# Two heads per slot, q in two f16 parts, and fewer DMAs for the attention rows of a fused attention and FFN block

## What is computed

```python
x = L0_attn_x                                  # (16, 256, 128) f32
xn = _layernorm(x, axis=-1)
x = x + attn(xn, ...) + ffn(xn, ...)
# attn: 16 heads of 8 dims, for each of the 16 batches
q, k, v = (split_heads(einsum('bsh,oh->bso', xn, w) * s + b) for each of q, k, v)
attn = softmax(einsum('bhqd,bhkd->bhqk', q, k) / sqrt(8), axis=-1)
ctx = einsum('bhqk,bhkd->bhqd', attn, v)       # then merged and sent through w_o, s_o, b_o
# ffn: three dense layers with weights of +1 and -1, 256(x, -x) -> 512 -> 512 -> 128
h = relu(s0 * h @ W0) * 2; h = relu(s1 * h @ W1) * 2; h = s2 * h @ W2
```

## Time and profile before

| what | us |
|---|---|
| median of three runs | 345.76 (343.56 to 347.13) |
| the profiled execution | 348.12 |
| its span, first to last instruction | 346.3 |
| busy: PE, DVE, ACT, POOL | 310.8, 281.3, 237.1, 107.5 |

### The profile page before, as it was taken

The page is one execution under the profiler, slowest core; times in us unless marked ns, Lnnn a source line. Parts: engine busy times, 40 slices in busy tenths (PEclk is TensorE's granted clock), DMA queues, the critical chain, the costliest instruction groups (busy, mean ns, idle before and its releaser), DMA issues.

```text
span 346.3 us, 9162 instructions
## 1 busy us (share of the span) xinstructions
PE 310.8 (90%) x3248; PEld 174.2 (50%) x3248; DVE 281.3 (81%) x655; ACT 237.1 (68%) x515; POOL 107.5 (31%) x186
## 2 busy tenths in 40 slices
PE   5957789998999999999999998999989999997792
PEld 5734445454554555564555545455645555553331
DVE  4737778888988898888989888988889988988722
ACT  2314286877778696968677785968777786956771
POOL 2332323323242432433232424324222424300000
PEclk9978989999999999999999999999999999999987
DMA  4231314031322313141313223131413223130001
GB/s 122 59 96 40 91 39 112 22 108 38 89 76 64 103 48 102 48 116 35 99 49 85 82 61 103 43 109 42 114 27 100 66 77 88 42 107 4 19 3 31
DMA packets 28415, 23.88 MB, mean 69 GB/s; under 512 B 5698, under 2 KB 25170, under 8 KB 28370
## 3 DMA queue, kind: packets, MB, share of 16 engines
q1 hardware_dynamic: 28370, 23.29, 25.1%
HBM read 15.47 MB, written 7.34 MB: 66 GB/s over the span
## 4 chain that ended last, share of the span: by engine, by line
PE 41%; SPq 26%; DMA 13%; ACT 7%; issue 6%; POOL 3%; DVE 3%; POOLq 0%; ACTq 0%; DVEq 0%
SPq L360 12%; PE st_bank L846 12%; PE ctx_bank L880 10%; DMA q_rows<-max_rows 10%; SPq L365 7%; PE work L938 5%; PE work L908 5%; PE work L894 4%; SPq L352 3%; DMA q_rows<-q_scratch 3%; SPq L392 3%; POOL q_part L325 3%; ACT probs L502 2%; PE work L928 2%; ACT q_part L556 2%
## 5 line engine op out<-in xcount | busy, mean ns | idle before, releaser
L502 ACT ACTIVATE probs<-st_bank 128x512 f32<-128x512 f32 x248 | 148.7, 603 | 67.8 <-PE st_bank L846 64.7
L647 DVE TENSOR_REDUCE neg_max<-s_bank 128x2 f32<-128x512 f32 x248 | 168.5, 683 | 25.3 <-PE s_bank L853 23.0
L846 PE MATMUL st_bank<-q_rows,k_rows 51*128 51x256 bf16 x496 | 94.3, 274 | 15.5 <-DMA q_rows<-max_rows 9.9
L853 PE MATMUL s_bank<-k_rows,q_rows 48*128 48x256 f16 x496 | 95.8, 276 | 3.9 <-DMA q_rows<-q_scratch 3.9
L880 PE MATMUL ctx_bank<-probs,v_ext 128*32 128x256 f32 x1024 | 69.8, 391 | 1.2 <-ACT probs L502 1.2
L846 PEld LDWEIGHTS st_bank<-q_rows,k_rows 51*128 51x128 f16 x496 | 28.9, 94 | 70.7 <-issue 34.3
L901 PE MATMUL work<-r_hi,w 128*128 128x256 f16 x256 | 59.6, 274 | 3.8 <-DVE r_lo L618 2.2
L901 PE MATMUL work<-r_lo,w 128*128 128x256 f16 x256 | 59.2, 272 | 0.0
L722 DVE STREAM_TRANSPOSE turned<-ctx_bank 128x256 f32<-128x256 f32 x64 | 28.6, 446 | 22.3 <-PE ctx_bank L880 21.1
L618 DVE SCALAR_TENSOR_TENSOR r_lo<-work,r_hi 128x512 f16<-128x512 f32 x64 | 43.5, 681 | 3.9 <-ACT r_hi L491 3.8
L491 ACT ACTIVATE r_hi<-work 128x512 f16<-128x512 f32 x64 | 38.3, 602 | 11.4 <-PE work L901 9.8
(11 more groups left out here) (97 smaller groups left out, 393.1 us busy)
## 6 DMA issues: line engine op xcount, KB each, us to landing
k_rows<-k_scratch SPq DMA_DIRECT2D x64, 96.0 KB
q_rows<-q_scratch SPq DMA_DIRECT2D x64, 96.0 KB
q_scratch<-q_part SPq DMA_DIRECT2D x48, 64.0 KB, 2.0
xin<-x SPq DMA_DIRECT2D x16, 128.0 KB, 2.1
k_scratch<-k_part SPq DMA_DIRECT2D x32, 64.0 KB, 2.0
out<-outs SPq DMA_DIRECT2D x16, 128.0 KB, 1.8
q_rows<-max_rows SPq DMA_DIRECT2D x64, 6.0 KB
w_sb<-w SPq DMA_DIRECT2D x1, 256.0 KB, 2.6
```

Of the source, the lines that this page charges most:

```text
L502: nc.scalar.activation(probs[head // GROUP % 2][:, head % GROUP, :, :].rearrange("p k q -> p (k q)"), exp_banks(s)[t % len(exp_banks(s))][ ...
L647: nc.vector.tensor_reduce(out=neg_max[:, t // HALF, t % 2, t % HALF // 2, :], in_=max_banks(s)[t % len(max_banks(s))][:, :].rearrange("p ( ...
L846: return mm(banks[t % len(banks)][:, kt * SEQ:(kt + 1) * SEQ], k[:, kt * P:(kt + 1) * P], q, start=True, stop=True)
L853: return mm(banks[t % len(banks)][:, qt * SEQ:(qt + 1) * SEQ], q[:, qt * P:(qt + 1) * P], k, start=True, stop=True)
```

## The change

- **Two heads a slot.** A step has 8 slots `j`. PE writes the scores of heads 2j and 2j+1 of lag 2 into one pair of banks `st_pair`, then those of lag 1 into one pair `s_pair`. ACT and DVE read 1024 elements at once. While both lags exist there is one pair for each, written again in the next slot once its reader is done; in steps with one lag only, two pairs alternate. The slot tables are gone, the work is written out by slot.
- **q in two f16 parts**, scaled by powers of two that are worked out from the weights at the start (`row_scales`, now some 17 small DVE operations and one more matmul of PE between them). Rows are 8 x 2 x 2 = 32, with maxima 34. Exp takes its scale from a tile.
- **Splits.** DVE casts q and k hi in one operation of 128 x 512, POOL subtracts both lo in one. ACT makes no parts.
- **DMAs.** Four stores (k and q of hi, then of lo) and four loads of 32 rows, all loads behind all stores. The x load stands ahead of `store_max` of half 1.
- **Maxima.** Three small operations on POOL, two f16 parts, 16 maxima rows for 2 row DMAs' sources.
- **Contexts.** Groups 0 and 1 lie side by side in the bank and are transposed at once (128 x 512), and so 2 and 3.

```diff
-QPARTS, KPARTS = 3, 2
-ROWS = DH * QPARTS * KPARTS
-MROWS = ROWS + QPARTS
+PARTS = 2
+ROWS = DH * PARTS * PARTS
+MROWS = ROWS + PARTS
...
+QUARTER = HALF // 2
+HROWS = PARTS * QUARTER * TT
...
-    q_scratch = nc.dram_tensor("q_scratch", (2 * DH, QPARTS, HALF, SEQ), bf16, kind="Internal").ap()
-    k_scratch = nc.dram_tensor("k_scratch", (2 * DH, KPARTS, HALF, SEQ), f16, kind="Internal").ap()
+    q_scratch = nc.dram_tensor("q_scratch", (2 * DH, PARTS, HALF, SEQ), f16, kind="Internal").ap()
+    k_scratch = nc.dram_tensor("k_scratch", (2, PARTS, DH, HALF, SEQ), f16, kind="Internal").ap()
...
+        def split_qk(s, engine, eng):
+
+            s.wait(eng, hi_ready, 1, 0, 1)
+            s.wait(eng, lo_stored, 16 * 2, 1, 16 * 2)
+            engine.tensor_tensor(qk_part[:, 1, :, :], qk[:, :, :], qk_part[:, 0, :, :], ALU.subtract
+                                 ).then_inc(lo_ready, 1)
...
                     s.wait(sp, rows_loaded, LOADS, 1, LOADS)
-                    for part, ready in ((0, k_hi_ready), (1, k_lo_ready)):
+                    for part, ready, stored in ((0, hi_ready, hi_stored), (1, lo_ready, lo_stored)):
                         s.wait(sp, ready, 1, 0, 1)
...
+                        sp.dma_start(k_scratch[:, part].rearrange("x d e t -> x (d e) t"), qk_part[:, part, 1, :]
+                                     ).then_inc(stored, 16)
+                        sp.dma_start(q_scratch[:, part], qk_part[:, part, 0, :]).then_inc(stored, 16)
+
+                    s.wait(sp, hi_stored, 32, 0, 32)
+                    s.wait(sp, lo_stored, 32, 0, 32)
+                    s.wait(sp, st_psum, HALF, 3, HALF)
+                    for par in range(2):
+                        k_src = k_scratch[par:par + 1].rearrange("x b d e t -> (b d) x (e t)")
+                        sp.dma_start(k_rows[s.third(0)][par * TILE:par * TILE + ROWS, :],
+                                     k_src.to_broadcast([PARTS * DH, PARTS, COLS])).then_inc(rows_loaded, 16)
+                    for par in range(2):
+                        q_src = q_scratch[par * DH:(par + 1) * DH].rearrange("d (x a) e t -> x (d a) (e t)", x=1)
+                        sp.dma_start(q_rows[s.third(0)][par * TILE:par * TILE + ROWS, :],
+                                     q_src.to_broadcast([PARTS, PARTS * DH, COLS])).then_inc(rows_loaded, 16)
...
+            def scores_for_exp(s, j):
+
+                if j % QUARTER == 0:
+                    s.wait(pe, max_rows_loaded[j // QUARTER], MAX_LOADS, 2, MAX_LOADS)
+                pairs = exp_pairs(s)
+                s.wait(pe, probs_ready, HALF, 2, j if j == 0 else j + 1 - len(pairs))
...
+                dst = pairs[j % len(pairs)]
+                for kt in range(TT):
+                    for par in range(2):
+                        q, k = (rows_of(rows, s.third(2), 2 * j + par, MROWS) for rows in (q_rows, k_rows))
+                        c = (TT * par + kt) * SEQ
+                        last = mm(dst[:, c:c + SEQ], k[:, kt * P:(kt + 1) * P], q, start=True, stop=True)
+                last.then_inc(st_psum, 1)
+
+            def scores_for_max(s, j):
+
+                if j == 0:
+                    s.wait(pe, rows_loaded, LOADS, 1, LOADS)
+                pairs = max_pairs(s)
+                s.wait(pe, max_ready, HALF, 1, j + 1 - len(pairs))
...
+            def split_max(s, lag, half):
+
+                full, part = neg_max[:, half], max_part[:, half]
+                s.wait(pool, max_ready, HALF, lag, QUARTER * (half + 1))
+                s.wait(pool, maxT_psum, 2, lag + 1, half + 1)
...
+                    if j == 1 and s.has(3):
+                        turn_context(s, 3, 1)
...
                         nc.vector.reciprocal(rden[:, :, :], turned[:, :, :, DH]).then_inc(rden_ready, 1)
...
+                    if j == 1 and s.has(0):
+                        s.wait(dve, qk_scaled, 2, 0, 2)
+                        s.wait(dve, hi_stored, 32, 1, 32)
+                        s.wait(dve, lo_ready, 1, 1, 1)
+                        nc.vector.tensor_copy(qk_part[:, 0, :, :], qk[:, :, :]).then_inc(hi_ready, 1)
...
+                    if j == 2 and s.has(0):
+                        s.wait(dve, l1_psum, 2, 1, 2)
+                        for k, name in enumerate(("l0a", "l0b")):
+                            s.wait(dve, r0_hi_ready, 2, 0, k + 1)
+                            relu_lo(k, psum(name), r0_hi, r0_lo, r0_ready)
```

More of the change, by code:

```diff
@@ L61 @@
 TURN = 32
[L68 to L82, removed]
+BANK = {"xT": 0, "qk": 0, "l0b": 0, "l1a": 0, "v": 0, "max1": 1, "l0a": 1, "l1b": 1, "l2": 2, "max0": 2, "o": 2}
 class Step:
@@ L502, in step @@
                         nc.scalar.activation(
-                            probs[head // GROUP % 2][:, head % GROUP, :, :].rearrange("p k q -> p (k q)"),
-                            exp_banks(s)[t % len(exp_banks(s))][:, :], ACT.Exp, scale=EXP_SCALE).then_inc(probs_ready, 1)
-                    if t == ACT_SLOT["ffn"] and s.has(1):
+                            probs[j // 2 % 2][:, j % 2 * 2:j % 2 * 2 + 2, :, :].rearrange("p h k q -> p (h k q)"),
+                            pairs[j % len(pairs)][:, :], ACT.Exp, scale=exp_scale[:, :]).then_inc(probs_ready, 1)
@@ new lines, in step @@
+                    if j == 0 and s.has(0):
+                        s.wait(act, xT_psum, 1, 0, 1)
+                        s.wait(act, v_psum, 1, 2, 1)
+                        s.wait(act, l0_psum, 2, 2, 2)
+                        b = psum("xT")[:, 0:SEQ]
+                        nc.scalar.activation(xT[s.par(0)][:, :], b, ACT.Copy, scale=X_UP).then_inc(xT_copied, 1)
+                        nc.scalar.activation(xT_hi[s.par(0)][:, :], b, ACT.Copy, scale=X_UP).then_inc(xT_copied, 1)
+                    if j == 1 and s.has(2):
+                        copy_max(s, 2, 1)
@@ new lines, in step @@
+                    if j == 1 and s.has(0):
+                        if s.first == 0:
+                            act.wait_ge(rows_scale_ready, 3)
+                        s.wait(act, qk_psum, 1, 0, 1)
+                        s.wait(act, lo_ready, 1, 1, 1)
+                        for n in range(2):
+                            nc.scalar.activation(qk[:, n, :], psum("qk")[:, n * SEQ:(n + 1) * SEQ], ACT.Identity,
+                                                 scale=rows_scale[:, n:n + 1], bias=rows_bias[:, n:n + 1]
+                                                 ).then_inc(qk_scaled, 1)
@@ L513, in step @@
                                              ).then_inc(ffn_ready, 1)
-                    for half in range(2):
-                        lag = 1 + half
-                        if t == ACT_SLOT[f"max{half}"] and s.has(lag):
-                            s.wait(act, maxT_psum, 2, lag, half + 1)
-                            s.wait(act, max_rows_loaded[half], MAX_LOADS, lag + 1, MAX_LOADS)
-                            src = psum(f"max{half}")[:, :].bitcast(bf16)
-                            nc.scalar.activation(max_rows[half][:, :], src[0:2 * HROWS, 0:P], ACT.Copy
-                                                 ).then_inc(max_rows_ready, 1)
@@ L686, in step @@
+                    if j == 3 and s.has(3):
                         s.wait(dve, ctxn_ready, 1, 3, 1)
@@ L699, in step @@
                         relu_lo(0, psum("l1a"), r1_hi, r1_lo, r1_ready)
[L700 to L708 removed]
+                    if j == 7 and s.has(3):
                         s.wait(dve, o_psum, 1, 3, 1)
@@ new lines, in scores_for_max @@
+            def scores_for_max(s, j):
+                if j == 0:
+                    s.wait(pe, rows_loaded, LOADS, 1, LOADS)
+                pairs = max_pairs(s)
+                s.wait(pe, max_ready, HALF, 1, j + 1 - len(pairs))
+                dst = pairs[j % len(pairs)]
+                for qt in range(TT):
+                    for par in range(2):
+                        q, k = (rows_of(rows, s.third(1), 2 * j + par, ROWS) for rows in (q_rows, k_rows))
+                        c = (TT * par + qt) * SEQ
+                        last = mm(dst[:, c:c + SEQ], q[:, qt * P:(qt + 1) * P], k, start=True, stop=True)
+                last.then_inc(s_psum, 1)
```

524 lines of the change are left out of this document (215 added, 309 removed).

## The result

The changed kernel takes 398.03 us (median of four runs, 393.99 to 403.21) against 346.44 us: 1.146 times as long, 95% interval 1.132 to 1.159. The forecast was 372 us, at most 388. The sign and the cause held, the size did not: 52 us were lost and I had found 26.

A forecast was written before the change was run, and what follows sets the result against it. Late q rows on two DMA engines were to bound each step: 20.2 us, 20.9 with the clock, for 19.2. Middle steps +23.8, ends +3.7, +1.8, -0.9, -2.3: +26.1, 374.2, from the median 372 us; range 346 to 388, eight in ten.

The forecast's parts named there:

- What bounds the loop: Middle steps, 19.2 us before: closed by a transfer, through projection, parts, stores, row loads and maxima rows, PE nearly full behind.
- Engine counts: DMAs use the largest number up to 16 dividing both sides' outermost counts: q loads and k stores 2, k loads 16.
- Until the parts are stored: From step start to parts in DRAM: hi ready at 5.25 us, all stored at 11.0 instead of about 9.7.
- The q loads' price: Row loads: 32 rows at 0.169 us on two engines, 5.4 us; maxima land at 20.1, a step of 20.2 us.
- The clock: PE idles over 2 us at step ends; low clock delays the projection 1.3 us in half the steps: 20.9 a step.
- The ends: First and last steps: step 0 +3.7 us, step 1 +1.8, step 16 -0.9, steps 17 and 18 -2.3.
- Rival 1: q loads not confined to two engines, rows not late, PE's 18.1 us a step decides: 326 us, chance 0.13.
- PE's own step: PE's work in a middle step: 16.5 us, 17.0 with gaps; 18.1 with waiting in the slots.
- fewer entries into this form: Score matmuls on PE: two heads of both kinds in a row save 1.6 us a step, between nothing and 1.6.
- the waits of the slots: One pair of banks: PE waits 0.7 us at slot 4 for DVE, 1.1 a step with other slots.
- Rivals 2 and 3: Confined but hidden by faster rows: 344 to 347 us, chance 0.04; slots bind on top: alone about 370, chance 0.05.

The follow-up runs named there:

- q_split: Changed kernel with each q load cut in two, 16 source rows to 16 destination rows without repeat: 338.48 us, ratio 0.976.
- q_inner: Changed kernel with the q loads' source written as 16 rows repeated inside instead of 2 outside, some scores wrong: 337.85 us, ratio 0.966.
- both: q_split and k_spread together on the changed kernel: 334.31 us, ratio 0.967.
- before_outer: Kernel before the change, its q loads taking 12 source rows repeated outside (2 x 12) instead of 24 once: 472.94 us, ratio 1.356.
- warm: Changed kernel with 12 identity transposes on PE at the start of each of steps 3 to 16, ahead of its wait for the maxima rows: 380.22 us.
- best2: q_split with the second `relu_lo` of layer 0 behind slot 3's reduce and POOL making the low parts ahead of ctxn: 331.78 us, ratio 0.950.
- q_first: Changed kernel with the two q loads issued ahead of the two k loads: 391.13 us.
- k_spread: Changed kernel with each k store cut in two, of 64 partitions each, q loads as they are: 398.90 us.
- pool_order: Changed kernel with POOL making the low parts ahead of ctxn: 398.33 us.
- best1: both with the second `relu_lo` of layer 0 moved from slot 2 to slot 3, behind its reduce: 332.01 us, ratio 0.950.
- best3: best2 with the k stores also cut in two: 335.80 us, ratio 0.961.

## Why the prediction was right in kind and short in size

*What bounds the loop.* Right: the chain runs through stores, row loads and maxima rows, and PE waits for the last of them at 14 of the 15 starts from step 2 to step 16.

*Engine counts.* Right to the packet. The rule worked out on the kernel before gives 1916 closing packets after: 3708 less 64 x 16 maxima rows, 512 and 256 leave 1916. It also gave 4668, 4156, 5628 and 5058 for q_split, q_inner, both and before_outer. The Trainium skill's sentence on a leading zero-stride broadcast (DMA: Bandwidth & Descriptors, rules for kernel authors), by which c copies outside confine a transfer to at most c engines, is what q_inner and before_outer show from both sides: 60 us gained and 123 lost by the place of a 2.

*Until the parts are stored.* Right: hi was forecast at 5.25 and stored from 5.54, all parts in DRAM at 11.0 against 10.8. The two-engine k stores are part of it, and hidden only in that spreading them costs SP as much.

*The q loads' price.* The rate of 0.169 us a row held (0.14 to 0.17). The fixed part failed: I had 7.6 us from the first q issue to the landing of the maxima (5.4 of rows, 0.3, 1.9), and 8.5 came (217.70 to 226.23). The difference lies ahead of the first row: in run warm the first q load is issued at 123.38, and the share stands at 0.12 to 0.14 only from 126 to 131. Even so the full-clock step of warm, 20.5, is 0.3 from the forecast 20.2: its first q load is issued 12.1 us into the step, where I had 12.5, and its maxima land 8.3 us after that.

*The clock.* This is the step that failed: "This 1.3 us is on the loop. I take it in half of the steps: 20.9 a step." The mechanism held, the size did not: nine of 14 steps ran to their projection at the low clock, or partly so, instead of seven, and the price of one was too small. I had taken it from one start in rows 9, where PE came back to full speed soon. Here the projection came up to 2.0 us late, and in seven of the nine its own four matmuls took 2.08 us instead of 1.13, so the first store was issued 6.9 to 8.5 us into such a step instead of 5.55. Against the 20.5 of late rows alone, a low step lasts 2.5 us more; over all 14 that is 1.6 us a step, where I had 0.7. The five full-clock steps last 0.9 more than 20.5, in which SP's k issues are 0.4 to 0.9 us slower: another 0.3 over the 14, which I had not priced. With the 0.3 of the point before, a step is 1.5 us longer than forecast. That is 14 x 1.5 = 21 us of the 29 between my 374.2 and the 403.2 of the profiled run, 13 of them the clock beyond the 0.7 a step that I had given it.

*The ends.* Steps 0 and 1 were nearly right (26.96 for 26.1, 21.28 for 21.0). The last three steps took 39.4 us for a forecast 32.8: the granted clock was 0.71 there. In q_split, with 0.97, the same steps take 33.5 us. So 5.9 of these 6.6 us go with the clock again, which I had not carried into the tail.

*Rival 1* (rows not late: 326 us) did not happen, but q_split and q_inner made its world: 338 us. PE's own step was too low in it. PE's busy time in a middle step goes from 18.3 us (256.29 / 14) to 17.9 in best2 (197.10 / 11), a saving of 0.4 for the forecast 1.6. The score matmuls of a step, each counted up to its own end or the next start, take 5.45 us before and 5.19 in best2, so the forecast 1.6 for fewer entries into this form is not borne out. PE alone needs 17.97 us where I had 17.0, and the waits of the slots 0.43 where I had 1.1. Both errors lean against each other: 18.40 for 18.1.

*Rivals 2 and 3.* No engine moved rows fast enough to hide them. The slots bind, but by 0.43 us, and not on top of the late rows: in the changed kernel PE has 1.4 to 3.6 us to spare at the end of each middle step but one. That one, from 250.19, I had no case for: its granted clock is 0.77, and PE is busy for all of its 22.2 us. At that clock PE's own work is as long as the late rows' step.

The four executions lie at 394 to 403 us and the range ended at 388. The main reason is that the range took in errors of the row price, of the slots and of the engines, but kept the clock at one number: of the 29 us, 13 in the middle steps and 5.9 in the last three are the clock's, and the 10 that remain would have stayed inside it.

## What to carry to other kernels

Read a DMA's engines from the outermost count of both sides before pricing its bytes: a repeat written outside made two 128 KB loads 5 us long together, and the same loads with their 16 rows outside cost the loop nothing. Where a change lets PE stand idle at a fixed place in each step, price the clock on the whole stretch from there to the first transfer, in most steps and in the tail too, and give the range a case for it. When the chain names a link, look for the one beside it: an earlier POOL split moved nothing, since the two-engine k stores ended just as late, and wider stores moved nothing, since SP's issues grew by what the data lost.

## What the runs showed that I had not expected

- Late rows and the low clock take turns. In the changed kernel and in q_first, each full-clock step of the middle is followed by one whose projection is late (q_first's last by a step without one); PE idles 1.8 to 3.6 us between them. In a low step PE's own work is longer, it idles less before the next start, and that one is often at full clock again. So the q loads issued 1.3 us earlier in q_first shortened single steps and nearly left the turns as they were. The turns are not strict: k_spread has two full-clock steps in a row twice, with 2.2 and 2.7 us of idle between them, and pool_order once, with 2.5.
- The last three steps, with the same work, follow the clock from run to run: 33.5 us at 0.97 (q_split), 34.9 at 0.92 (best2), 36.0 at 0.83 (best1), 38.3 at 0.74 (best3), 39.9 at 0.66 (k_spread).
- Work without use shortens a run: 12 transposes of the identity a step, 168 in all, take 18 us off the changed kernel.
- SP's issue of the same two k loads takes 1.25 us in some steps and 1.7 to 2.1 in others (rows of SP above: 2.13 and 1.25): in the changed kernel in its five full-clock steps and in none of the other middle ones, in warm in three of 16 steps, in best2 in none. Full clock is not the condition: pool_order has 2.5 us in a low step and k_spread 2.0. The cause stays open.
- Of two stores to DRAM on the same queue, the later one waits: a q store that spans 16 engines lands 3.1 us after its issue behind the two-engine k stores and 2.1 us behind spread ones.
